# Queries and keys of a hybrid kernel: three bfloat16 parts against two float32r parts, heads in the halves of the rows

## What is computed

```python
# 1. convolutional attention, one head, 16 channels of queries and keys
q = einsum('bcn,dc->bnd', xf, wq) + bq;  k = einsum('bcn,dc->bdn', xf, wk) + bk[:, None]
attn = softmax(einsum('bnd,bdm->bnm', q, k));  x = x + v @ attn.T
# 2. on layer-normed tokens: global attention (8 heads of 16), 1024 x 1024 scores each,
scores = einsum('bqhd,bkhd->bhqk', q, k) / sqrt(16);  o = softmax(scores) @ v
#    local attention (4 heads, window 5), a fused two-layer MLP, layer norm, an FFN, layer norm
# 3. a routed mixture of 8 experts over all 8192 tokens, scattered back and added
```

## Time and profile before

| | |
|---|---|
| median of 3 runs | 1704.99 us (1702.29 to 1707.94) |
| the profiled execution, its own time | 1713.91 us |
| its span | 1711.8 us |
| mean granted TensorE clock | 0.947 |
| TensorE matmul busy | 1547.5 us, 90% |
| VectorE busy | 1369.4 us, 80% |
| ScalarE busy | 1023.9 us, 60% |
| GpSimd busy | 628.9 us, 37% |

### The profile page before, as it was taken

How to read it: one execution, slowest core, us unless ns; L and a number is a source line. 1 busy time by engine, 2 the same in 40 slices (tenths; PEclk the granted TensorE clock), 3 DMA queues, 4 the chain that set the end, 5 groups by cost and what they waited for, 6 DMA issues and landing times.

```text
span 1711.8 us, 24948 instructions
## 1 busy us (share of the span) xinstructions
PE 1547.5 (90%) x8470; PEld 759.4 (44%) x8470; DVE 1369.4 (80%) x2806; ACT 1023.9 (60%) x1947; POOL 628.9 (37%) x1027
## 2 busy tenths in 40 slices
PE   4858899999999999999998999999989998879993
PEld 1523433443444345434543364425433433349992
DVE  4169798789988998998888988998789883747984
ACT  1411566576767676867675768676666677415443
POOL 4112210104532444245224352454245455324562
PEclk8776899999999999999999999999999998989997
DMA  3165642053305321542045113621262111033335
GB/s 81 51 169 185 205 123 77 27 138 95 114 18 154 101 97 37 156 130 81 27 124 155 44 61 107 164 73 30 73 179 85 54 69 43 10 82 107 111 119 212
DMA packets 126988, 169.89 MB, mean 99 GB/s; under 512 B 16144, under 2 KB 88773, under 8 KB 126862
## 3 DMA queue, kind: packets, MB, share of 16 engines
q1 hardware_dynamic: 117742, 157.44, 31.0%
q0 software_dynamic: 4608, 7.30, 1.3%
q10 hardware_dynamic: 4512, 3.56, 0.7%
HBM read 107.17 MB, written 62.52 MB: 99 GB/s over the span
## 4 chain that ended last, share of the span: by engine, by line
PE 57%; DVE 18%; ACT 8%; DMA 5%; POOL 5%; issue 4%; SPq 2%; ACTq 1%; POOLq 0%; DVEq 0%
PE bank L1621 9%; PE bank L1590 8%; PE bank L1609 8%; PE bank L1545 7%; DVE gmax L2242 5%; PE bank L1855 4%; DVE cmax L2181 3%; PE bank L1464 3%; ACT prob L1991 2%; PE bank L1658 2%; PE bank L1537 2%; PE bank L1648 2%; DMA gparts_d<-parts 2%; PE bank L1559 2%; DMA kv_d<-lqkv 2%
## 5 line engine op out<-in xcount | busy, mean ns | idle before, releaser
L1991 ACT ACTIVATE prob<-bank 128x512 f32<-128x512 f32 x1024 | 572.3, 595 | 281.9 <-PE bank L1609 279.3
L2242 DVE TENSOR_REDUCE gmax<-bank 128x1 f32<-128x512 f32 x1024 | 656.1, 681 | 45.4 <-PE bank L1590 43.8
L1590 PE MATMUL bank<-k_stack,q_stack 96*128 96x512 bf16 x1024 | 400.8, 397 | 36.1 <-DVE gmax L2242 19.1
L1609 PE MATMUL bank<-q_stack,k_stack 99*128 99x512 bf16 x1024 | 388.1, 387 | 25.5 <-ACT prob L1991 17.9
L1621 PE MATMUL bank<-prob,v_tok 128*32 128x512 f32 x2048 | 280.2, 621 | 0.0
L1378 POOL TENSOR_TENSOR lprod<-ql_tok,kv_win 128x640 f32<-128x640 f32 x64 | 100.5, 1591 | 359.4 <-DMA ql_tok<-ql_d 344.1
L1590 PEld LDWEIGHTS bank<-k_stack,q_stack 96*128 96x128 bf16 x1024 | 100.5, 99 | 276.4 <-DVE gmax L2242 171.8
L1609 PEld LDWEIGHTS bank<-q_stack,k_stack 99*128 99x128 bf16 x1024 | 99.8, 99 | 187.1 <-ACT prob L1991 131.3
L1385 POOL TENSOR_TENSOR lprod<-ls,kv_win 128x640 f32<-128x640 f32 x64 | 81.7, 1298 | 264.8 <-DVE ls L2298 264.8
L1545 PEld LDWEIGHTS bank<-cv_tok,cprob 128*128 128x128 f32 x960 | 117.6, 197 | 27.0 <-DVE t_tok L2209 14.4
L1545 PE MATMUL bank<-cv_tok,cprob 128*128 128x129 f32 x960 | 125.2, 284 | 2.3 <-ACT cprob L1939 1.4
(11 more groups left out here) (291 smaller groups left out, 2471.4 us busy)
## 6 DMA issues: line engine op xcount, KB each, us to landing
kv_win<-kv_d SPq DMA_DIRECT2D x32, 1280.0 KB, 5.7
kv_d<-lqkv SPq DMA_DIRECT2D x64, 128.0 KB, 2.2
gparts_d<-cprob SPq DMA_DIRECT2D x24, 256.0 KB
gparts_d<-parts SPq DMA_DIRECT2D x24, 256.0 KB
q_stack<-gparts_d SPq DMA_DIRECT2D x32, 192.0 KB, 3.1
k_stack<-gparts_d SPq DMA_DIRECT2D x16, 384.0 KB, 5.5
rows_d<-rows SPq DMA_DIRECT2D x10, 528.0 KB, 6.0
cprob<-rows_d SPq DMA_DIRECT2D x8, 660.0 KB, 5.6
```

The costliest lines, as they stand in the source:

```text
L1590: mm(max_ps[max_bank(n)][:, :], q_stack[quad][0:KROWS, h, i * P:(i + 1) * P], key_slot(b, quad)[0:KROWS, h, j * HN:(j + 1) * HN], start=Tr ...
L1609: mm(score_ps[n % 2][:, :], key_slot(b, quad)[0:KM, h, j * P:(j + 1) * P], q_stack[quad][0:KM, h, half * HN:(half + 1) * HN], start=True, ...
L1991: nc.scalar.activation(prob[:, g % 2, h, :], score_ps[n % 2][:, :], ACT.Exp).then_inc(exp_made, 1)
L2242: v.tensor_reduce(gmax[:, h, i, j:j + 1], max_ps[max_bank(n)][:, :], AX.X, ALU.max)\
```

## The change

Queries and keys are split in two float32r parts (the rounded value and the remainder). Three products of parts (48 rows, KROWS) and two rows of negative maxima (KM = 50) make a stack; stacks of two heads lie in rows 0 to 63 and 64 to 127 of one tile. For the convolution the two halves of the rows hold the two halves of the keys, and the queries twice. The weights of its projections are repeated so that the matmul writes every row of the stack, ScalarE evicts all rows in place, and VectorE overwrites the remainder's rows with one operation a row group; the transfers are gone. For the global heads ScalarE writes the first part, VectorE the remainder from the same PSUM tile, and two parts of float32 are stored and loaded (four transfers a stack, not three). `max_pair` issues the matmuls of two heads, one in each half of the rows, back to back, waits for the banks of both, and VectorE reduces both in one step. `neg_parts` has three operations. Four small loads of biases and three memsets come in the opening, the bfloat16 identity goes. The planner's durations are other ones, `SHIFTS` is empty, and maxima count as one bank use a pair. The output of the kernel is the same quantity.

```diff
-Q_PART = [0, 1, 2, 0, 1, 0]
-K_PART = [2, 1, 0, 1, 0, 0]
-RUNS = [(0, 0, 3), (3, 0, 2), (5, 0, 1)], [(0, 0, 3), (3, 1, 2), (5, 2, 1)]
-TERMS = len(Q_PART)
-KROWS = TERMS * D
-KM = KROWS + 3
+Z = P // 2
+KROWS = 3 * D
+KM = KROWS + 2
+RUNS = [(0, 0, 1), (1, 0, 2)], [(0, 0, 2), (2, 0, 1)]
+STACK_LOADS = 2 * len(RUNS[0])
 GROUPS = 2 * NT
 TILES = GROUPS * QH
-NEG_STEPS = 5
+NEG_STEPS = 3
+PAIRS = TILES // 2
...
-    "max_tile": [("pe", 0.22, 0.22), ("dve", 0.6, 0.1)],
-    "guard": [("dve", 1.15, 0.1), ("pe", 0.11, 0.3)],
-    "guard_rows": [("dve", 0.2, 0.2), ("sp", 1.9, 3.5)],
+    "max_pair": [("pe", 0.3, 0.25), ("dve", 0.63, 0.0), ("dve", 0.63, 0.1)],
+    "guard": [("dve", 0.75, 0.1), ("pe", 0.15, 0.3)],
+    "guard_rows": [("dve", 0.2, 0.2), ("sp", 1.3, 3.5)],
...
+    "conv_q": [("pe", 0.9, 0.3), ("act", 0.56, 0.2), ("dve", 1.38, 0.1)],
+    "conv_k": [("pe", 0.9, 0.3), ("act", 0.56, 0.2), ("dve", 1.38, 0.1)],
+    "store_parts": [("sp", 1.3, 4.3)],
...
 SHIFTS = [
-    ("conv_qk", 1, -12.0), ("local_qkv", 0, -3.0), ("a_channels", 5, -12.0), ("norm_u", 6, -3.0),
...
-    ("chain keys", 0, -12.0), ("fuse1", 0, -3.0), ("conv_stacks", 5, 12.0),
 ]
...
+            if step not in begun.setdefault(engine, set()):
+                orders.setdefault(engine, []).append(step)
+                begun[engine].add(step)
...
-TAIL_PS, MAX_PS, SCORE_PS = ("tail", 1), ("max", 3), ("score", 2)
-def split_of(s, a, w, low, after):
-    s.add("split", a, ("split", w), (a, after))
-    s.add("split", a, low, (a, ("split", w)))
+TAIL_PS, MAX_PS, SCORE_PS = ("tail", 1), ("max", 1), ("score", 2)
+WEIGHT_PS = ("weight", 3)
...
+        s.add("head", a, ("conv_q", h), (a, ("load_x",)), (a - 1, ("conv_exp", 1, NT - 1)), banks=ps)
+    s.add("head", a, ("conv_k",), (a, ("load_x",)), banks=ps)
...
+    for p in range(PAIRS):
+        s.add("maxima", a, ("max_pair", quad, p), (a, ("key_stacks", quad)),
+              (a, ("query_stacks", quad, p // (PAIRS // 2))), banks=MAX_PS)
+    s.add("maxima", a, ("guard", quad), (a, ("max_pair", quad, PAIRS - 1)), banks=MAX_PS)
...
-    parts_d = nc.dram_tensor("parts_d", [B, 3, 2 * D, N], BF16).ap()
-    gparts_d = nc.dram_tensor("gparts_d", [B, 2, HEADS, 3, D, N], BF16).ap()
+    gparts_d = nc.dram_tensor("gparts_d", [B, 2, HEADS, 2, D, N], F32).ap()
...
-            return m // NT, HT * half + m % NT // 2, m % 2
+            return m % 2, m // NT // 2, HT * half + m // 4 % HT, m // 2 % 2
...
-        FIRST_LOADS = 2 + 1 + 11 + 1
+        FIRST_LOADS = 2 + 1 + 8 + 1 + 4
...
-            def split_low(b, w):
-                after(sp, split_step, b * 9 + 3 * w + 3)
-                for s in range(3):
-                    sp.dma_start(gparts_d[b, w - 1, :, s], split_home(b, w)[0][:, s, :])\
-                      .then_inc(gsplit_out[w - 1], 16)
-            def split_low0(b):
-                after(sp, split_step, b * 9 + 3)
-                sp.dma_start(parts_d[b].rearrange("s c n -> c s n"), split_home(b, 0)[0][0:2 * D]).then_inc(split_out, 16)
-            def conv_stacks(b):
-                if not (isinstance(b, int) and b == 0):
-                    head_filled(sp, b - 1, ("conv_exp", 1, NT - 1))
-                if b:
-                    after(sp, split_out, b * 16)
-                    source = parts_d[b].rearrange("s c n -> c s n")
-                else:
-                    after(sp, split_step, 3)
-                    source = parts[0:2 * D, :, :]
-                for r in range(TERMS):
-                    sp.dma_start(cq_stack[D * r:D * r + D, :], source[0:D, Q_PART[r], :])\
-                      .then_inc(cstacks_in, 16)
...
+            def store_parts(b, w):
+                for h in range(2):
+                    head_done(sp, b, ("global_qk", w - 1, h))
+                for s in range(2):
+                    sp.dma_start(gparts_d[b, w - 1, :, s], split_home(b, w)[s]).then_inc(gsplit_out[w - 1], 16)
...
-                for r, part, k in RUNS[w]:
-                    sp.dma_start(st[D * r:D * (r + k), :, n],
-                                 src[D * part:D * (part + k), quad * QH:(quad + 1) * QH, n]).then_inc(in_sem, 16)
+                src = gparts_d[b, w].rearrange("(q j z) s d n -> q z (s d) j n", q=QUADS, z=2)
+                for z in range(2):
+                    for r, part, k in RUNS[w]:
+                        sp.dma_start(st[Z * z + D * r:Z * z + D * (r + k), :, n].bitcast(F32),
+                                     src[quad, z, D * part:D * (part + k), :, n]).then_inc(in_sem, 16)
...
+            def conv_q(b, h):
+                ps, full = head_fill(pe, b, ("conv_q", h))
                 after(pe, x_in, (b + 1) * 16)
-                mm(ps[0:2 * D, :], cqkT[:, :], x_cm[:, h * HN:(h + 1) * HN], start=True, stop=True).then_inc(full, 1)
+                for z in range(2):
+                    last = mm(ps[rows_of(z, Z), :], cqw[:, :], x_cm[:, h * HN:(h + 1) * HN], start=True, stop=True)
+                last.then_inc(full, 1)
...
-                mm(ps[:, :], cq_stack[0:KROWS, i * P:(i + 1) * P], ck_stack[0:KROWS, j * HN:(j + 1) * HN],
+                mm(ps[:, :], cq_stack[rows_of(j), i * P:(i + 1) * P], ck_stack[rows_of(j), :],
...
-            def max_tile(b, quad, n):
-                max_fill(b, quad, n)
-                if n == 0:
-                    after(pe, keys_in[quad], (b + 1) * 3 * 16)
-                if n % (TILES // 2) == 0:
-                    after(pe, queries_in[quad][n // (TILES // 2)], (b + 1) * 3 * 16)
-                h, i, j = max_at(n)
-                mm(max_ps[max_bank(n)][:, :], q_stack[quad][0:KROWS, h, i * P:(i + 1) * P],
-                   key_slot(b, quad)[0:KROWS, h, j * HN:(j + 1) * HN], start=True, stop=True).then_inc(max_full, 1)
+            def max_pair(b, quad, p):
+                if p == 0:
+                    after(pe, keys_in[quad], (b + 1) * STACK_LOADS * 16)
+                if p % (PAIRS // 2) == 0:
+                    after(pe, queries_in[quad][p // (PAIRS // 2)], (b + 1) * STACK_LOADS * 16)
+                for n in (2 * p, 2 * p + 1):
+                    max_fill(b, quad, n)
+                for n in (2 * p, 2 * p + 1):
+                    z, w, i, j = max_at(n)
+                    mm(max_ps[max_bank(n)][:, :], q_stack[quad][rows_of(z), w, i * P:(i + 1) * P],
+                       key_slot(b, quad)[rows_of(z), w, j * HN:(j + 1) * HN], start=True, stop=True).then_inc(max_full, 1)
...
+                k = rows_of(h % 2, KM)
+                mm(score_ps[n % 2][:, :], key_slot(b, quad)[k, h // 2, j * P:(j + 1) * P],
+                   q_stack[quad][k, h // 2, half * HN:(half + 1) * HN], start=True, stop=True).then_inc(score_full, 1)
...
-                to(parts_[0:rows_, part_at(w, 0), n], ps[0:rows_, :], bias=bias, scale=scale)
-                to(rest[0:rows_, n], ps[0:rows_, :], bias=bias, scale=scale)\
-                    .then_inc(free, 1)
...
+            def conv_q(b, h):
+                ps, _ = head_read(act, b, ("conv_q", h))
+                if b:
+                    head_filled(act, b - 1, ("conv_exp", 1, NT - 1))
+                to(cq_stack[:, h * HN:(h + 1) * HN], ps[:, :], bias=cols[:, COL["cq"]:COL["cq"] + 1]).then_inc(chi_made, 1)
...
+                to(split_home(b, 1 + w)[0][:, h * HN:(h + 1) * HN].bitcast(F32R), ps[:, :], bias=bias).then_inc(ghi_made, 1)
...
-                v.tensor_tensor(rest[r, :], rest[r, :], parts_[r, part_at(w, 0), :], ALU.subtract).then_inc(split_step, 1)
...
-                v.tensor_tensor(parts_[r, part_at(w, 2), :], rest[r, :], parts_[r, part_at(w, 1), :], ALU.subtract)\
...
+            def remainder(dst, ps, bias, part):
+                return v.scalar_tensor_tensor(dst, ps, bias, part, ALU.add, ALU.subtract)
+            def conv_q(b, h):
+                ps, free = head_read(dve, b, ("conv_q", h))
+                dve.wait_ge(chi_made, 3 * b + h + 1)
+                n = slice(h * HN, (h + 1) * HN)
+                for z in range(2):
+                    r = slice(Z * z + 2 * D, Z * z + 4 * D)
+                    remainder(cq_stack[r, n], ps[r, :], cols[r, COL["cq"]:COL["cq"] + 1], cq_stack[r, n].bitcast(F32))\
+                        .then_inc(clo_made if z == 0 else free, 1)
...
+            def global_qk(b, w, h):
+                ps, free = head_read(dve, b, ("global_qk", w, h))
+                dve.wait_ge(ghi_made, 4 * b + 2 * w + h + 1)
+                hi, lo = split_home(b, 1 + w)
+                n = slice(h * HN, (h + 1) * HN)
+                bias = hcols[:, 0:1] if w == 0 else cols[:, COL["gk"]:COL["gk"] + 1]
+                remainder(lo[:, n].bitcast(F32R), ps[:, :], bias, hi[:, n]).then_inc(free, 1)
...
                 v.tensor_reduce(neg, maxima, AX.X, ALU.max, negate=True).then_inc(step, 1)
-                v.tensor_reduce(parts_[:, 0, :], maxima, AX.X, ALU.max, negate=True).then_inc(step, 1)
+                v.tensor_reduce(parts_[0].bitcast(F32R), maxima, AX.X, ALU.max, negate=True).then_inc(step, 1)
                 after(dve, step, n + 2)
```

(17 more changed lines are left out.)

279 lines of the change are left out of this document (129 added, 150 removed).

## The result

The changed kernel takes **1920.9 us** (median of four runs, 1904.8 to 1930.3) against 1706.2: 12.5% slower, ratio 1.125 with a 95% interval of 1.117 to 1.133. Its profiled execution has a span of 1903.0 us, 191 more than before.

A forecast was written before the change was run, and what follows sets the result against it. It took TensorE, in order, as the bound (57% of the chain), VectorE close behind. Terms -13 - 24 - 2 + 12 = -27 took the profiled 1713.9 to 1687, the median from 1705 to 1679 us; own range 1655 to 1705, whole 1640 to 1735.

The forecast's parts named there:

- Rival A: TensorE, middle: switching between half-row and full-width matmuls eats the pairs' gain, 0.23 us a step, +84 on TensorE; 1734 us, chance 0.15.
- point of decision: Switch price on TensorE, 0.13 us a step, from which the gains of all parts are gone.
- Part 1: Opening: first maximum near 20 us instead of 28.8, first head maximum near 95, key store earlier; -13 us, ends -5 and -18.
- the forecast 87: Opening: the keys' store issued near 87 us instead of 91.80, after one eviction and one remainder; -5 us.
- The four terms of the recorded sum: Opening: earlier first maximum -8.5, added loads, memsets and weight copy +1, earlier key store -5, larger store and more issues +1.5.
- +1.5: Opening: the store moves 1 MB for 0.75 and each stack load has four issues for three; +1.5 us.
- Part 2: TensorE, middle: float32r +0.015 us a tile, maximum pairs 0.30 for 0.44; sum -42 us, of which the chain gives -24.
- Part 3: VectorE: operations removed, remainders of 0.70 us added, `neg_parts` shorter; some -10 us, of which the chain gives -2.
- Rival B: VectorE is the true bound, so TensorE's freed time turns to waits; no change, 1702 us, chance 0.20.
- Part 4: Order: `SHIFTS` emptied and pairs asking for two of three banks can stop VectorE; +12 us, ends 0 and +45.
- Rival D: VectorE starves at the pairs or the raw order is much worse: +45 for the order, 1711 us, chance 0.10.
- the 80 that were to show D: Sign in VectorE's wait for maxima: 41.5 us before, over it by 10 or so forecast, 80 or more for Rival D.

The follow-up runs named there:

- The ladder: Series of kernels between the kernel before (1707.0 us) and the changed kernel (1920.9 us); each step is a difference of two medians with the steps above in place.

## Why the prediction was wrong

**The step that failed is the missing one**: no term of the sum and no rival priced TensorE's clock. I read 0.99 in the earlier trace rows, took every duration at full speed, and never asked what the chip grants when matmuls read 48 rows. The profile puts a number beside it: 1903.0 x (1 - 0.862) = 263 us of full speed not granted, against 91 before. That is 172 us more, and not all of it is lost time. Two pairs of profiled executions say what such a microsecond is worth: from the changed kernel to the one on 64 rows 81 us came back in the clock and 52 in the span, and in the kernel before from 35 to 64 rows 141 and 114. By these shares (0.64 and 0.81) the clock explains an estimated 110 to 140 of the 191 us. The ladder bounds it from the other side: on full rows, with the clock back (0.96 over the execution), the changed kernel still takes 1787.1 us. So clock and switches together, less the overlap, are 133 us, and the other steps of the ladder 81.

**Rival A had another part.** The switch of form was named and given 0.15 and a price of 0.23 us a step from a product with the values. The price was from the wrong row: column strips pay a change of form in any case (0.35 with float32r on all rows), and the full-width steps pay 0.40 with a float32r matmul, 0.21 with a bfloat16 one between them in the runs of TensorE alone, about 0.30 in the changed kernel's middle. 364 x 0.40 = 146 us on TensorE in the middle is an upper bound, since some steps follow each other. The rule of the Trainium skill, TensorEngine Tiling (Array Packing), Key Properties, is that changing the tiling mode drains the engine. A price at each change to and from the full width agrees with it; the draining itself no run here shows. Against it I had put that the 0.09 and 0.14 us were partly stagger; that was not tried. Its point of decision, 0.13 us a step, is passed two to three times over, but its 1734 us was far from enough without the clock.

**Part 1.** Projections ended near 15.6 us (forecast 16.0), but all six remainders run one after the other and I had put only two behind the last eviction; TensorE then stood three times for VectorE (1.21, 0.91 and 0.89 us). Timeline of batch 0, TensorE and VectorE:

```profile
14.64 1.02 PE L1486 MATMUL bank<-x_cm,ckw 128*64 128x512 f32 x4
16.87 0.66 PE L1434 MATMUL bank<-ident,x_cm 128*128 128x128 f32 x4 [1.21 <-DVE cq_stack L2135]
...
19.98 2.05 PE L1492 MATMUL bank<-cvw,x_cm 128*128 128x128 f32 x16 [0.89 <-DVE ck_stack L2135]
21.96 0.50 PE L1503 MATMUL bank<-ck_stack,cq_stack 48*128 48x512 f32 x2
...
15.28 3.10 DVE L2135 SCALAR_TENSOR_TENSOR cq_stack<-bank,cols,cq_stack 32x512 fp32r<-32x512 f32 x4 [3.92 <-ACT cq_stack L1871]
18.41 1.52 DVE L2135 SCALAR_TENSOR_TENSOR ck_stack<-bank,cols,ck_stack 16x512 fp32r<-16x512 f32 x2
```

The first maximum came at 21.96 for 20, still 6.9 us earlier than before. The parts of the keys were complete at 81.96, 9.8 us earlier than before (91.76). There the gain was lost. SyncE issues two loads (`t_old`, `a_old`) from 81.00 us on. In the kernel before they went out at about the same time (81.24), ahead of both stores of parts; now they stand between the two, and hold SyncE until 85.3. So the store of the keys went out at 85.39 and 87.53. That this is near the forecast 87 is luck: the forecast left the last eviction near 85.71, where it was before, and it began at 80.42. Then the load of the keys waits for the store's transfer and goes out only at 99.21.

```profile
80.35 1.61 DVE L2135 SCALAR_TENSOR_TENSOR split_x<-bank,cols,parts 128x512 fp32r<-128x512 f32 x2 [0.80 <-ACT parts L1871]
81.00 2.57 SPq L1120 DMA_DIRECT2D t_old<-kept_d  x1
83.61 1.68 SPq L1121 DMA_DIRECT2D a_old<-kept_d  x1
85.39 2.09 SPq L1127 DMA_DIRECT2D gparts_d<-parts  x1
87.53 0.58 SPq L1127 DMA_DIRECT2D gparts_d<-split_x  x1
99.21 1.73 SPq L1145 DMA_DIRECT2D k_stack<-gparts_d  x4
...
107.85 0.80 PE L1573 MATMUL bank<-k_stack,q_stack 48*128 48x512 f32 x2 [15.38 <-DMA k_stack<-gparts_d]
```

In the kernel before the load of the keys goes out 8.1 us after the store's first issue, here 13.8. So the first head maximum ran at 107.8, not 95 to 96: of -13 us 1.4 were there. (The four terms of the recorded sum, -8.5, +1, -5 and +1.5, add up to -11, not -13.) The term "+1.5" for a store of a third more bytes and four issues for three was the wrong size. The two loads ahead of the store took 8.4 and 10.8 us to land, for 4.0 and 4.8 in the kernel before, so all transfers were slow there; that they shared the queue with the store is the likely reason, and was not tried.

**Part 2.** Float32r was put at 0.015 us a tile. With the chain's 0.57 on it, as the forecast had it, that is 0.009 of time. For the heads it measured 19 us over 2048 tiles, 0.009 each, so that term was right; for the convolution 11 to 13 us over 256 tiles, 0.04 to 0.05 each, five times the term. Pairs: 0.34 us instead of 0.30 to the next matmul at full clock, in the bounds (the 255 us rows); what they are worth with everything else in place is 66 us. What the term left out is the price of a pair beside full-width steps: 0.16 us more than two matmuls on all rows.

**Part 3.** Remainders took 0.74 to 0.75 us for 0.70. VectorE did not come near being the bound: 910 us busy in the middle for 1026. Rival B is out.

**Part 4.** +12 was put for the list and the pairs; they measured +15 and +31, together my upper end of +45. Rival D, given 0.10 and 1711 us, so had the size of this term, 46, in part by luck: the 31 were measured on full rows, where a pair brings no overlap. VectorE waits 90.7 us for maxima in the middle, past the 80 that were to show D, but the sign was a poor one: on 35 rows, with no pair at all, it waits 88.4. A slower TensorE alone brings it about.

## What to carry to other kernels

Before matmuls are cut to a part of the array's rows, count the full-width steps between them and price the clock as well as the switch: a stream on 48 rows of one half ran at half the clock, and this kernel's middle fell from 0.99 to 0.89. Overlap pays in long runs of alternating halves (0.114 us each here) and beside column strips, where a second half-row matmul was free, not where one pair stands between full-width steps. If halves must be, read all of the half: rows of zeros, at the price of two small transfers a load, gave back 68 us. A step that asks for two of three buffers at once can cost by itself (31 us here, the plan's order included), which a test with the overlap taken out shows. And choose signs that only one rival can bring about.
